# A recommender tower with embedding look-ups by matmul: the last two tables are looked up in batch halves

## The chip, the cores and the metric

One core of a Trainium2 chip runs the whole kernel. The metric is the device time of one execution in microseconds (us). The core has a tensor engine (PE, whose weight loads are shown apart as PEld), a vector engine (DVE), a scalar engine (ACT), GpSimd (POOL), and a sync engine (SP) that issues DMAs; they run side by side and wait for each other through semaphores.

## What is computed

For a batch of 512 items, 26 rows are looked up by id, one in each of 26 tables of 128 columns, and stacked with a dense vector of 128 values to 27 features. The products of all pairs of features (351 of them) and the dense vector go through three layers:

```python
e = jnp.stack([tbl_0[ids[:, 0]], ..., tbl_25[ids[:, 25]]], axis=1)
all_emb = jnp.concatenate([bottom_output[:, None, :], e], axis=1)
gram = jnp.einsum('bfd,bgd->bfg', all_emb, all_emb)
z = gram[:, _TRIU_I, _TRIU_J]
h = jnp.concatenate([z, r_bottom_output], axis=1)
h = jnp.maximum(h @ W_top1 + b_top1, 0.0)      # 479 -> 512
h = jnp.maximum(h @ W_top2 + b_top2, 0.0)      # 512 -> 256
y = h @ W_top3                                 # 256 -> 1
```

All is in float32.

## The kernel before

The batch is cut into four tiles of 128 items. `features` (in SBUF) holds for each item its 27 features, with the 128 columns on the partitions.

**Picked tables.** The twelve tables of 1000 rows (`PICKED`) are not gathered. SP loads each whole table in order (L175); ACT rounds it to `table_hi` (L319) and DVE subtracts that to get `table_lo` (L221). The look-up is a matmul with a one-hot matrix that DVE (L236, L239) and ACT (L322, L328) make from the ids: PE's `pick(i)` runs 8 matmuls of 512 columns with `table_hi` (L425) and 8 with `table_lo` (L434), all into one of two PSUM banks, and ACT's `pick_out` (L333) copies the bank to `features`. The tables are handled in couples that share a one-hot buffer. Buffers of `table_hi` and `table_lo` alternate, so that their writers wait for the pick two tables earlier (`picked_done`).

**Gathered tables.** The other fourteen tables are gathered row by row by POOL: for each tile, four groups (`TURNS`: 4, 4, 4 and 2 tables), one indirect DMA per table (L204), 56 in all, in the order of tiles. Gathers of tiles 2 and 3 reuse the buffers of tiles 0 and 1 and wait until those groups are turned. PE turns each group with transposes (`turn(t, g)`, L450), and ACT or DVE copies the result into `features` (L216). `AFTER_PICK` says behind which pick a turn stands in PE's order, `TAIL_TURNS` gives the order of the later ones; ACT copies the turns of `AFTER_PICK`, DVE those of the tail. The pair turns `("z", t)` of the tail are in the same numbering, since all turns share two PSUM banks.

**Products and layers.** `products(t, half)` runs two matmul instructions (27 columns) for each of 64 items of a tile (L463). When both halves are done, DVE transposes them in blocks (`grams_out`, L261 and L263), ACT takes the wanted pairs out (`bands_out`, L347), PE turns these (`pairs_turn`, L475), DVE copies them (L213), and the layers follow: `layer1` (L481), `layer2` (L501), `layer3` (L508), with ACT's copies (L352, L357, L362) behind each. A float32 matmul of the code is two matmul instructions on PE, each with its own weight load.

**Order.** Each engine runs its program in the order in which it is written out by hand; there is no planner. PE's order is at the end of the tensor block: the twelve picks with turns behind some of them, then products, turns, pair turns and layers interleaved. PE runs every instruction in that order.

Of the kernel before, what the change touches and what calls it, by code (L numbers as in the profile page):

```python
# [17 lines left out]
BIAS_ROW = CHUNK_ROWS  # L18
PICKED = [1, 2, 4, 5, 11, 13, 14, 16, 22, 23, 24, 25]
PICKS = len(PICKED)  # L20
COUPLES = PICKS // 2
GATHERED = [f for f in range(TABLES) if f not in PICKED]
ORDER = PICKED + GATHERED
PICK_ROWS = 1000
RPP = BIG_RPP = -(-PICK_ROWS // 128)
# [10 lines left out]
def rpp(i):  # L36
    return BIG_RPP if i // 2 in BIG_COUPLES else RPP
# [8 lines left out]
def dve_onehots(j):  # L46

    return sum((2 if k == 0 else 1) * (rpp(2 * k) - 1) for k in range(j))


def act_onehots(j):
    return sum(2 if k == 0 else 1 for k in range(j))


AFTER_PICK = {2: [(0, 0)], 3: [(0, 1)], 4: [(0, 2)], 5: [(0, 3)], 6: [(1, 0)], 8: [(1, 1)], 9: [(1, 2)], 10: [(1, 3)],
              11: [(2, 0)]}
TAIL_TURNS = [(2, 1), ("z", 0), (2, 2), (2, 3), (3, 0), ("z", 1), (3, 1), (3, 2), (3, 3), ("z", 2), ("z", 3)]
TURN_ORDER = [rows for i in range(PICKS) for rows in AFTER_PICK.get(i, [])] + TAIL_TURNS
PLACE = {what: n for n, what in enumerate(TURN_ORDER)}
BY_ACT = [n < len(TURN_ORDER) - len(TAIL_TURNS) for n in range(len(TURN_ORDER))]  # L60
# [3 lines left out]
def dlrm_tower(nc, bottom_turned, ids, picked_ids, picked, tables, w1, w2, b2, w3, out):  # L64
# [3 lines left out]
    with ExitStack() as ctx:  # L68
# [40 lines left out]
        pick_ps = mlp_ps  # L109
# [4 lines left out]
        def onehot_of(i, c):  # L114
            return onehot[i // 2 % 2][:, c, :, :]
# [103 lines left out]
        def _(dve):  # L219
# [31 lines left out]
            def turn_out(n):  # L251
                dve.wait_ge(turned, n + 1)
                copy_turned(nc.vector.tensor_copy, n).then_inc(turn_dve, 1)

            def grams_out(t):

                dve.wait_ge(prods_done, t + 1)
                by_second = prod_ps[t % 2][:].rearrange("p m c -> p c m")
                if t >= 1:
                    dve.wait_ge(bands_ready, 2 * t)  # L260
                nc.vector.transpose(grams[:, 0:FEATURES - 1, :], by_second[:, 1:FEATURES, :]  # L261
                                    ).then_inc(grams_ready, 1)
                nc.vector.transpose(grams[:, FEATURES - 1:, :], by_second[:, 0:BANDS, :]  # L263
                                    ).then_inc(grams_ready, 1)
# [8 lines left out]
            for i in range(PICKS):  # L273
                pick_operands(i)
            dve.wait_ge(fills_ready, 4)
            grams_out(0)
            turn_out(PLACE[(2, 1)])
            turn_out(PLACE[("z", 0)])
            grams_out(1)
            turn_out(PLACE[(2, 2)])  # L280
            turn_out(PLACE[(2, 3)])
            turn_out(PLACE[(3, 0)])
            turn_out(PLACE[("z", 1)])
            grams_out(2)
            turn_out(PLACE[(3, 1)])
            turn_out(PLACE[(3, 2)])
            turn_out(PLACE[(3, 3)])
            turn_out(PLACE[("z", 2)])
            grams_out(3)
            turn_out(PLACE[("z", 3)])  # L290

# [1 line left out]
        def _(act):  # L293
# [34 lines left out]
                    nc.scalar.activation(onehot[j % 2][:, 0, :, :], distance[:], ACT.Relu, bias=1.0, scale=-4.0  # L328
                                         ).then_inc(onehot_act, 1)

            def pick_out(i):
                act.wait_ge(picked_done, i + 1)
                nc.scalar.copy(features[:, :, 1 + i, :],  # L333
                               pick_ps[i % 2][:].rearrange("p a (b i) -> p (a b) i", i=2)
                               ).then_inc(picks_ready, 1)

            def turn_out(n):
# [30 lines left out]
            for i in range(PICKS + 2):  # L368
                if i < PICKS:
                    table_high(i)  # L370
# [5 lines left out]
                if 1 <= i <= PICKS:  # L376
                    pick_out(i - 1)
            act.wait_ge(fills_ready, 4)
            act.wait_ge(mlp_in, 48)
            act.wait_ge(onehot_act, act_onehots(COUPLES))  # L380
            bands_out(0)
            bands_out(1)
            h1_out(0, 0)
            h1_out(0, 1)
# [20 lines left out]

        @block.tensor
        def _(pe):
            def pick(i):

                if i == 0:  # L410
                    pe.wait_ge(first_hi_ready, 1)
                else:
                    pe.wait_ge(hi_ready, i + 1)
                if i >= 2:
                    pe.wait_ge(picks_ready, i - 1)
                acc = pick_ps[i % 2][:].rearrange("p a b -> p (a b)")
                for n, c in enumerate(places(i)):
                    if i == 0 and n == HALF:
                        pe.wait_ge(hi_ready, 1)
                    before = dve_onehots(i // 2) + (RPP - 1 if i == 1 else 0)  # L420
                    if c == 0:
                        pe.wait_ge(onehot_act, i + 1 if i < 2 else act_onehots(i // 2 + 1))
                    elif i % 2 == 0 or i == 1:
                        pe.wait_ge(onehot_ready, before + n + 1)
                    nc.tensor.matmul(acc, table_hi[i % 2][:, c, :], onehot_of(i, c)[:, i % 2, :],  # L425
                                     start=(n == 0), stop=False)
                if i == 0:
                    pe.wait_ge(first_lo_ready, 1)
                else:
                    pe.wait_ge(lo_ready, i + 1)  # L430
                for n, c in enumerate(places(i)):
                    if i == 0 and n == HALF:
                        pe.wait_ge(lo_ready, 1)
                    last = nc.tensor.matmul(acc, table_lo[i % 2][:, c, :], onehot_of(i, c)[:, i % 2, :],  # L434
                                            start=False, stop=(n == rpp(i) - 1))
                last.then_inc(picked_done, 1)

            def copied(n):
# [76 lines left out]
            for i in range(PICKS):  # L515
                pick(i)
                for rows_of in AFTER_PICK.get(i, []):
                    if rows_of == (0, 0):
                        pe.wait_ge(ident_ready, 1)
                    turn(*rows_of)  # L520
            pe.wait_ge(fills_ready, 4)
            pe.wait_ge(bottom_ready, 1)
            pe.wait_ge(picks_ready, PICKS)
            products(0, 0)
            products(0, 1)
            turn(2, 1)
            products(1, 0)
            pairs_turn(0)
            products(1, 1)
            turn(2, 2)  # L530
            turn(2, 3)
            pe.wait_ge(w1_in, 16 * (CHUNKS + 1))
            pe.wait_ge(mlp_in, 48)
            layer1(0)
            turn(3, 0)
            products(2, 0)
            pairs_turn(1)
            layer2(0)
            layer3(0)
            products(2, 1)  # L540
            turn(3, 1)
            layer1(1)
            turn(3, 2)
            turn(3, 3)
            products(3, 0)
            pairs_turn(2)
            layer2(1)
            layer3(1)
            products(3, 1)
            layer1(2)  # L550
            pairs_turn(3)
# [54 lines left out]
```

## Time and profile before

| | |
|---|---|
| timed runs | 142.22, 143.40, 146.07 us; median 143.4 |
| profiled execution | 139.8 us, span 138.0 us |
| PE busy | 101.3 us (73%), 1520 matmuls |
| PE weight loads busy | 84.2 us (61%) |
| DVE, ACT busy | 58.1 us (42%), 49.5 us (36%) |
| POOL busy | 62.6 us (45%), 56 gathers |
| HBM read | 15.00 MB, 109 GB/s over the span |

The profile is of one execution. Its own time is a little more than its span, which counts from the first to the last instruction. Busy times of engines overlap; an engine's busy share over the whole span says little where the kernel has stages. Matmuls are pipelined and the ends of their records are modelled, so that a mean duration of one matmul is more than what it adds to a sequence: for the pace, take the start of a group and the start of the next. "Issue" as what ended a wait means that the profile shows nothing that the engine waited for.

### The profile page before, as it was taken

The numbers are of one execution on the slowest core, as the hardware profiler recorded it, in microseconds if no ns is written. First come the engines' busy times: TensorE is split into PE (matmuls) and PEld (weight loads), VectorE is DVE, ScalarE is ACT, GpSimd is POOL, SyncE is SP. The second block draws the span as 40 slices with busy tenths as digits, with TensorE's granted clock in tenths as the row PEclk, the third lists the DMA queues.
The fourth block names the chain that finished last, engine by engine and source line by source line (L and its number), as shares of the span: only waits on it lengthen the run. The fifth ranks groups of instructions, "written<-read, shape, count | busy, mean of one in ns | idle before, by whom it ended". The sixth has DMA issues, their size and how long they took to land.

```text
span 138.0 us, 3425 instructions
## 1 busy us (share of the span) xinstructions
PE 101.3 (73%) x1520; PEld 84.2 (61%) x1520; DVE 58.1 (42%) x87; ACT 49.5 (36%) x79; POOL 62.6 (45%) x63
## 2 busy tenths in 40 slices
PE   6998989999999969942111111556599976999994
PEld 6965558888888848821101000455499876989792
DVE  5799999599798971000000000014172062141000
ACT  4449648779495991130000000003031222124222
POOL 2388787887888788778777773000000000000000
PEclk9999999999999999997555555557999999999999
DMA  4895987985983982112211221000000000000000
GB/s 68 301 416 199 318 276 226 274 301 189 229 322 108 329 285 62 46 57 57 57 45 50 57 57 38 5 5 0 5 5 5 5 0 5 5 5 0 5 0 1
DMA packets 6369, 15.23 MB, mean 110 GB/s; under 512 B 1745, under 2 KB 2257, under 8 KB 6354
## 3 DMA queue, kind: packets, MB, share of 16 engines
q1 hardware_dynamic: 4418, 11.07, 23.6%
q0 software_dynamic: 1792, 3.67, 9.6%
q10 hardware_dynamic: 144, 0.26, 1.3%
q8 instruction: 12, 0.20, 0.6%
q14 instruction: 3, 0.02, 0.0%
HBM read 15.00 MB, written 0.00 MB: 109 GB/s over the span
## 4 chain that ended last, share of the span: by engine, by line
PE 38%; issue 28%; POOL 22%; DMA 8%; ACT 1%; DVE 1%
POOL rows L204 22%; PE prod_ps L463 11%; PE mlp_ps L481 11%; PE mlp_ps L501 5%; DMA rows<-in_tbl_dram,ids_all 5%; PE turn_ps L450 3%; DMA ids_all<-in_ids_dram 3%; PE mlp_ps L425 3%; PE mlp_ps L434 3%; PE turn_ps L475 1%; ACT h L357 1%; PE mlp_ps L508 1%; DVE features L216 1%; ACT distance L362 0%
## 5 line engine op out<-in xcount | busy, mean ns | idle before, releaser
L204 POOL DMA_INDIRECT rows<-in_tbl_dram,ids_all x56 | 61.8, 1104 | 20.8 <-issue 16.8
L463 PE MATMUL prod_ps<-features 128*27 128x27 f32 x1024 | 16.4, 203 | 29.9 <-issue 28.8
L463 PEld LDWEIGHTS prod_ps<-features 128*27 128x27 f32 x1024 | 13.5, 117 | 33.1 <-issue 31.7
L425 PE MATMUL mlp_ps<-onehot,table_hi 128*128 128x512 f32 x96 | 26.2, 408 | 1.0 <-ACT table_hi L319 0.5
L261 DVE STREAM_TRANSPOSE grams<-prod_ps 128x832 f32<-128x832 f32 x4 | 4.2, 1050 | 49.3 <-PE prod_ps L463 49.3
L434 PE MATMUL mlp_ps<-onehot,table_lo 128*128 128x512 f32 x96 | 24.2, 394 | 0.4 <-issue 0.4
L239 DVE TENSOR_SCALAR onehot<-ids_wide,row_of 128x1024 fp32r<-128x1024 int32 x35 | 23.7, 746 | 0.0
L434 PEld LDWEIGHTS mlp_ps<-onehot,table_lo 128*128 128x128 f32 x96 | 17.8, 188 | 5.1 <-issue 1.1
L425 PEld LDWEIGHTS mlp_ps<-onehot,table_hi 128*128 128x128 f32 x96 | 17.1, 188 | 6.0 <-DVE onehot L239 1.7
L347 ACT COPY bands<-grams 128x117 f32<-128x117 f32 (+1 forms) x8 | 4.0, 506 | 44.6 <-DVE grams L261 44.3
L221 DVE TENSOR_TENSOR table_lo<-table_raw,table_hi 128x1024 fp32r<-128x1024 f32 (+1 forms) x13 | 14.6, 1134 | 3.9 <-issue 3.9
L319 ACT CAST table_hi<-table_raw 128x1024 fp32r<-128x1024 f32 (+1 forms) x12 | 12.1, 1011 | 4.4 <-DMA table_raw<-in_picked_dram 3.5
L333 ACT COPY features<-mlp_ps 128x512 f32<-128x512 f32 x12 | 7.9, 656 | 12.9 <-PE mlp_ps L434 7.0
L481 PE MATMUL mlp_ps<-pairs,w_sb 128*128 128x128 f32 x96 | 11.4, 275 | 0.0
L481 PEld LDWEIGHTS mlp_ps<-pairs,w_sb 128*128 128x128 f32 x96 | 11.0, 192 | 0.0
L450 PE MATMUL turn_ps<-ident,rows 128*128 128x128 f32 x56 | 9.1, 287 | 1.1 <-DMA rows<-in_tbl_dram,ids_all 1.1
L450 PEld LDWEIGHTS turn_ps<-ident,rows 128*128 128x128 f32 x56 | 6.9, 146 | 2.7 <-DMA rows<-in_tbl_dram,ids_all 1.6
L501 PE MATMUL mlp_ps<-h,w_sb 128*128 128x128 f32 x64 | 8.1, 277 | 0.0
L501 PEld LDWEIGHTS mlp_ps<-h,w_sb 128*128 128x128 f32 x64 | 7.5, 192 | 0.2 <-ACT h L352 0.2
L357 ACT ACTIVATE h<-mlp_ps,b_sb 128x128 f32<-128x128 f32 x8 | 2.9, 367 | 10.5 <-PE mlp_ps L501 10.5
L216 DVE COPY features<-turn_ps 128x512 f32<-128x512 f32 (+1 forms) x7 | 4.0, 600 | 5.7 <-PE turn_ps L450 5.7
L514 PE MATMUL turn_ps<-h 128*128 128x128 f32 x28 | 5.7, 393 | 1.1 <-DVE h L266 1.1
(32 smaller groups left out, 61.8 us busy)
## 6 DMA issues: line engine op xcount, KB each, us to landing
table_raw<-in_picked_dram SPq DMA_DIRECT2D x11, 512.0 KB
ids_wide<-in_picked_ids_dram SPq DMA_DIRECT2D x5, 512.0 KB
w_sb<-in_W_top_dram SPq DMA_DIRECT2D x4, 256.0 KB
rows<-in_tbl_dram,ids_all POOLq DMA_INDIRECT x56
table_raw<-in_picked_dram SPq DMA_DIRECT2D x2, 256.0 KB, 4.6
w_sb<-in_W_top_dram SPq DMA_DIRECT2D x1, 512.0 KB
ids_wide<-in_picked_ids_dram ACTq DMA_DIRECT2D x1, 256.0 KB, 4.4
ids_wide<-in_picked_ids_dram SPq DMA_DIRECT2D x1, 256.0 KB
```

The lines of the kernel that those rows point to most:

```text
L204: nc.gpsimd.indirect_dma_start(out=rows[t % 2][:, slot - FIRST_G, :], out_offset=None, in_=tables[table], in_offset=bass.IndirectOffsetOnA ...
L221: return nc.vector.tensor_tensor(table_lo[i % 2][:, begin:end, :], table_raw[i % RAWS][:, begin:end, :], table_hi[i % 2][:, begin:end, :]. ...
L239: nc.vector.tensor_scalar(onehot_of(i, c), ids_wide[j % 2][:], row, None, ALU.is_equal).then_inc(onehot_ready, 1)
L319: nc.scalar.copy(table_hi[i % 2][:, 0:end, :], table_raw[i % RAWS][:, 0:end, :]).then_inc(hi_ready, 1)
L333: nc.scalar.copy(features[:, :, 1 + i, :], pick_ps[i % 2][:].rearrange("p a (b i) -> p (a b) i", i=2)).then_inc(picks_ready, 1)
L425: nc.tensor.matmul(acc, table_hi[i % 2][:, c, :], onehot_of(i, c)[:, i % 2, :], start=(n == 0), stop=False)
L434: last = nc.tensor.matmul(acc, table_lo[i % 2][:, c, :], onehot_of(i, c)[:, i % 2, :], start=False, stop=(n == rpp(i) - 1))
L450: last = nc.tensor.transpose(turn_ps[n % 2][:, i, :], rows[t % 2][:, slot - FIRST_G, :], ident[:])
L463: last = nc.tensor.matmul(prod_ps[t % 2][32 * s:32 * s + FEATURES, m, 0:FEATURES], item, item, start=True, stop=True)
L481: return nc.tensor.matmul(mlp_ps[n // 2][:, n % 2, :], w1_sb[:, c, 128 * n:128 * n + 128], rhs, start=start, stop=stop, skip_group_check=True)
L501: last = nc.tensor.matmul(mlp_ps[m][:, 2, :], w2_sb[:, c, 128 * m:128 * m + 128], h1[:, c, :], start=(c == 0), stop=(c == 3))
L514: nc.tensor.matmul(turn_ps[0][:, 0, :], h1[:, 0, :], h1[:, 0, :], start=True, stop=True)
```

## The change

Of the twelve picks, the first ten stay whole. The last two are each cut into two halves of the batch (256 columns); the order of the parts is: table 10 first half, table 11 first half, table 10 second half, table 11 second half. `pick` becomes `pick_high` and `pick_low`, and the four pieces of the second halves (8 matmuls each) are spread: one ahead of the products of tile 0, the others between products of tiles 0 and 1. Three turns of tile 1 move one pick forward, the turn (2, 0) is now copied by DVE, and the turns of tile 3, the pair turns and the products (3, 0) change their places in the tail. Products (3, 0) now stand directly ahead of products (3, 1).

```diff
+WHOLE = PICKS - 2
+PARTS = [(i, 0, 2) for i in range(WHOLE)] + [(WHOLE, 0, 1), (WHOLE + 1, 0, 1), (WHOLE, 1, 2), (WHOLE + 1, 1, 2)]
+SIDE = 256
...
-AFTER_PICK = {2: [(0, 0)], 3: [(0, 1)], 4: [(0, 2)], 5: [(0, 3)], 6: [(1, 0)], 8: [(1, 1)], 9: [(1, 2)], 10: [(1, 3)],
-              11: [(2, 0)]}
-TAIL_TURNS = [(2, 1), ("z", 0), (2, 2), (2, 3), (3, 0), ("z", 1), (3, 1), (3, 2), (3, 3), ("z", 2), ("z", 3)]
+AFTER_PICK = {2: [(0, 0)], 3: [(0, 1)], 4: [(0, 2)], 5: [(0, 3)], 6: [(1, 0)], 7: [(1, 1)], 8: [(1, 2)], 9: [(1, 3)]}
+TAIL_TURNS = [(2, 0), (2, 1), ("z", 0), (2, 2), (2, 3), ("z", 1), (3, 0), (3, 1), ("z", 2), (3, 2), (3, 3), ("z", 3)]
...
@@ DVE @@
             dve.wait_ge(fills_ready, 4)
+            turn_out(PLACE[(2, 0)])
             grams_out(0)
...
-            turn_out(PLACE[(3, 0)])
             turn_out(PLACE[("z", 1)])
             grams_out(2)
+            turn_out(PLACE[(3, 0)])
             turn_out(PLACE[(3, 1)])
+            turn_out(PLACE[("z", 2)])
             turn_out(PLACE[(3, 2)])
             turn_out(PLACE[(3, 3)])
-            turn_out(PLACE[("z", 2)])
             grams_out(3)
@@ ACT @@
-            def pick_out(i):
-                act.wait_ge(picked_done, i + 1)
-                nc.scalar.copy(features[:, :, 1 + i, :],
-                               pick_ps[i % 2][:].rearrange("p a (b i) -> p (a b) i", i=2)
+            def pick_out(part):
+                i, begin, end = PARTS[part]
+                act.wait_ge(picked_done, part + 1)
+                nc.scalar.copy(features[:, SIDE // 2 * begin:SIDE // 2 * end, 1 + i, :],
+                               pick_ps[i % 2][:, 2 * begin:2 * end, :].rearrange("p a (b i) -> p (a b) i", i=2)
                                ).then_inc(picks_ready, 1)
...
+            pick_out(WHOLE + 1)
+            pick_out(WHOLE + 2)
             act.wait_ge(fills_ready, 4)
             act.wait_ge(mlp_in, 48)
             act.wait_ge(onehot_act, act_onehots(COUPLES))
             bands_out(0)
+            pick_out(WHOLE + 3)
             bands_out(1)
@@ PE @@
+            def acc(i, begin, end):
+                return pick_ps[i % 2][:, 2 * begin:2 * end, :].rearrange("p a b -> p (a b)")
+
+            def pick_high(part):
+                i, begin, end = PARTS[part]
...
+                if part >= 2:
+                    pe.wait_ge(picks_ready, part - 1)
...
+                    nc.tensor.matmul(acc(i, begin, end), table_hi[i % 2][:, c, :], onehot_of(i, c)[:, i % 2, SIDE * begin:SIDE * end],
+                                     start=(n == 0), stop=False, skip_group_check=True)
...
+            pick_high(WHOLE)
+            pick_low(WHOLE)
+            pick_high(WHOLE + 1)
+            pick_low(WHOLE + 1)
+            turn(2, 0)
+            pick_high(WHOLE + 2)
             pe.wait_ge(fills_ready, 4)
             pe.wait_ge(bottom_ready, 1)
-            pe.wait_ge(picks_ready, PICKS)
+            pe.wait_ge(picks_ready, WHOLE + 2)
             products(0, 0)
+            pick_low(WHOLE + 2)
             products(0, 1)
+            pick_high(WHOLE + 3)
             turn(2, 1)
             products(1, 0)
+            pick_low(WHOLE + 3)
             pairs_turn(0)
             products(1, 1)
             turn(2, 2)
             turn(2, 3)
...
+            pe.wait_ge(picks_ready, WHOLE + 4)
             layer1(0)
-            turn(3, 0)
             products(2, 0)
             pairs_turn(1)
             layer2(0)
             layer3(0)
             products(2, 1)
+            turn(3, 0)
             turn(3, 1)
             layer1(1)
+            pairs_turn(2)
             turn(3, 2)
             turn(3, 3)
-            products(3, 0)
-            pairs_turn(2)
             layer2(1)
             layer3(1)
+            products(3, 0)
             products(3, 1)
             layer1(2)
             pairs_turn(3)
```

## Rows read from the trace of the kernel before

**Rows 1.** The page's part 2: busy tenths of the span in 40 slices.

```profile
PE   6998989999999969942111111556599976999994
...
POOL 2388787887888788778777773000000000000000
PEclk9999999999999999997555555557999999999999
```

**Rows 2.** Busy time by stage: stretch, length, busy us (count) of each engine, granted clock.

```profile
core 0: us, PE busy (x) PEld busy (x) DVE busy (x) ACT busy (x) POOL busy (x), PEclk, DMA share, GB/s
59.40:88.40 29.00, 4.96 (x73) 3.16 (x73) 0.00 (x0) 0.35 (x1) 18.88 (x20) 0.58 0.18 48
88.40:100.70 12.30, 7.95 (x453) 7.01 (x454) 3.24 (x5) 1.04 (x2) 0.00 (x0) 0.75 0.02 5
100.70:138.00 37.30, 32.94 (x745) 29.96 (x743) 8.99 (x15) 10.03 (x26) 0.00 (x0) 1.00 0.01 3
```

**Rows 3.** The waits of PE: us in total, times, longest us.

```profile
PE prod_ps L463 <- issue: 28.8, 24, 2.6
```

**Rows 4.** PE's timeline: start us, us, what, count, idle before it.

```profile
45.34 2.10 PE L425 MATMUL mlp_ps<-onehot,table_hi 128*128 128x512 f32 x8
47.27 1.99 PE L434 MATMUL mlp_ps<-onehot,table_lo 128*128 128x512 f32 x8
50.40 0.66 PE L450 MATMUL turn_ps<-ident,rows 128*128 128x128 f32 x4 [1.14 <-DMA rows<-in_tbl_dram,ids_all]
50.81 2.09 PE L425 MATMUL mlp_ps<-onehot,table_hi 128*128 128x512 f32 x8
...
54.69 2.07 PE L425 MATMUL mlp_ps<-onehot,table_hi 128*128 128x512 f32 x8
...
59.43 0.49 PE L463 MATMUL prod_ps<-features 128*27 128x27 f32 x37 [0.41 <-issue]
...
85.59 0.20 PE L463 MATMUL prod_ps<-features 128*27 128x27 f32 x1 [2.59 <-issue]
...
88.39 1.92 PE L463 MATMUL prod_ps<-features 128*27 128x27 f32 x143 [0.46 <-issue]
91.73 0.69 PE L463 MATMUL prod_ps<-features 128*27 128x27 f32 x41 [1.41 <-issue]
92.35 1.12 PE L450 MATMUL turn_ps<-ident,rows 128*128 128x128 f32 x4
93.39 1.23 PE L463 MATMUL prod_ps<-features 128*27 128x27 f32 x82
95.92 0.60 PE L463 MATMUL prod_ps<-features 128*27 128x27 f32 x46 [1.29 <-issue]
...
96.96 0.86 PE L463 MATMUL prod_ps<-features 128*27 128x27 f32 x78
99.47 0.63 PE L463 MATMUL prod_ps<-features 128*27 128x27 f32 x50 [1.64 <-issue]
...
104.84 1.28 PE L463 MATMUL prod_ps<-features 128*27 128x27 f32 x128
...
109.10 1.26 PE L463 MATMUL prod_ps<-features 128*27 128x27 f32 x122
...
112.25 0.49 PE L481 MATMUL mlp_ps<-bottom_t,w_sb 128*128 128x128 f32 x3 [0.74 <-issue]
...
117.17 1.28 PE L463 MATMUL prod_ps<-features 128*27 128x27 f32 x128 [1.09 <-DVE features L216]
```

**Rows 5.** The chain that ended last, one piece, and POOL's timeline, last gather.

```profile
43.77 6.59 DMA rows<-in_tbl_dram,ids_all
83.25 0.94 POOL L204 DMA_INDIRECT rows<-in_tbl_dram,ids_all  x1 [0.30 <-issue]
```

**Rows 6.** DMA queues: whole span, then 58 to 89 us, then 89 to 90 us.

```profile
q8 instruction: 12, 0.20, 0.6%
...
q0 software_dynamic: 705, 1.44, 17.9%
...
q8 instruction: 1, 0.02, 5.8%
```

**Rows 7.** The chain again: lengths of layer 1, layer 2 and a pair turn.

```profile
118.45 0.52 PE turn_ps L475 x3
118.97 1.80 PE mlp_ps L501 x16
...
122.69 3.77 PE mlp_ps L481 x32
```

More of the change, by code:

```diff
@@ L367, in _ @@
             act.wait_ge(minus_row_ready, 1)
-            for i in range(PICKS + 2):
-                if i < PICKS:
-                    table_high(i)
+            for i in range(PICKS):
+                table_high(i)
                 if i == 3:
@@ L375, in _ @@
                     turn_out(PLACE[rows_of])
-                if 1 <= i <= PICKS:
+                if 1 <= i:
                     pick_out(i - 1)
+            pick_out(WHOLE + 1)
+            pick_out(WHOLE + 2)
             act.wait_ge(fills_ready, 4)
@@ L407, in _ @@
         def _(pe):
-            def pick(i):
+            def acc(i, begin, end):
+                return pick_ps[i % 2][:, 2 * begin:2 * end, :].rearrange("p a b -> p (a b)")
+            def pick_high(part):
+                i, begin, end = PARTS[part]
                 if i == 0:
                     pe.wait_ge(first_hi_ready, 1)
-                else:
+                elif begin == 0:
                     pe.wait_ge(hi_ready, i + 1)
-                if i >= 2:
-                    pe.wait_ge(picks_ready, i - 1)
-                acc = pick_ps[i % 2][:].rearrange("p a b -> p (a b)")
+                if part >= 2:
+                    pe.wait_ge(picks_ready, part - 1)
                 for n, c in enumerate(places(i)):
@@ L419, in pick, with pick_low @@
                         pe.wait_ge(hi_ready, 1)
-                    before = dve_onehots(i // 2) + (RPP - 1 if i == 1 else 0)
-                    if c == 0:
+                    ready = dve_onehots(i // 2) + (RPP - 1 if i == 1 else 0)
+                    if c == 0 and begin == 0:
                         pe.wait_ge(onehot_act, i + 1 if i < 2 else act_onehots(i // 2 + 1))
[L423 to L426, printed above, removed]
+                    elif begin == 0 and (i % 2 == 0 or i == 1):
+                        pe.wait_ge(onehot_ready, ready + n + 1)
+                    nc.tensor.matmul(acc(i, begin, end), table_hi[i % 2][:, c, :], onehot_of(i, c)[:, i % 2, SIDE * begin:SIDE * end],
+                                     start=(n == 0), stop=False, skip_group_check=True)
+            def pick_low(part):
+                i, begin, end = PARTS[part]
                 if i == 0:
                     pe.wait_ge(first_lo_ready, 1)
-                else:
+                elif begin == 0:
                     pe.wait_ge(lo_ready, i + 1)
@@ L433, in pick @@
                         pe.wait_ge(lo_ready, 1)
-                    last = nc.tensor.matmul(acc, table_lo[i % 2][:, c, :], onehot_of(i, c)[:, i % 2, :],
-                                            start=False, stop=(n == rpp(i) - 1))
+                    last = nc.tensor.matmul(acc(i, begin, end), table_lo[i % 2][:, c, :], onehot_of(i, c)[:, i % 2, SIDE * begin:SIDE * end],
+                                            start=False, stop=(n == RPP - 1), skip_group_check=True)
                 last.then_inc(picked_done, 1)
@@ L514, in _ @@
                 nc.tensor.matmul(turn_ps[0][:, 0, :], h1[:, 0, :], h1[:, 0, :], start=True, stop=True)
-            for i in range(PICKS):
-                pick(i)
+            for i in range(WHOLE):
+                pick_high(i)
+                pick_low(i)
                 for rows_of in AFTER_PICK.get(i, []):
```

## The prediction

> **What bounds the kernel now.** I read the time first: the profiled execution took 139.8 us, of which the span is 138.0 and 1.8 lies around it; the median of the three timed runs is 143.4, which is 3.6 above it. Any change of the span that I work out is added to 143.4.
>
> The slices of the page come next [rows 1]. TensorE (PE) is 80 to 90% busy up to slice 16, nearly idle in slices 17 to 24, and dense again to the end; its granted clock halves (2.4 to 1.2 GHz) inside that hole and comes back behind it. GpSimd (POOL) is busy until the hole is nearly over. The table by stage says the same in us [rows 2]: from 59.4 to 88.4 PE is busy for 5.0 of 29.0 us, with DVE and ACT idle; the stage 88.4 to 100.7 (products of tiles 0 and 1) is 65% busy at a mean clock of 0.75; from 100.7 on PE is busy for 32.9 of 37.3 us at the full clock. The waits of PE [rows 3] put 28.8 us on the products line, released by "issue", that is, by nothing that the profile shows.
>
> The timeline of PE shows how it begins [rows 4]. 37 matmuls of the first half of tile 0's products run in 0.49 us, then single matmuls or threes follow at distances of 0.7 us or multiples of it, down to one in 1.4 to 2.8 us, and at 88.39 suddenly 143 run in 1.92 us. All wait for nothing that another engine computes. I call this the **crawl**: 35 pairs of weight load and matmul in 28.5 us. It begins when ACT's last copies are done and it ends 4.2 us after POOL's last gather leaves its engine (83.25 + 0.94 = 84.19) [rows 5]. Between 58 and 89 us the DMA engines carry the gathers and nothing else [rows 6].
>
> Behind it is a second limit, visible at 90.3, 94.6, 97.8 and 111.5 us. Between two such gaps lie 41 + 4 + 82 = 127 matmuls, and 46 + 3 + 78 = 127 [rows 4]. With their weight loads that is about 256 instructions, and the instruction queue moved 12 packets for 0.20 MB, 16 KB each, one at 89 to 90 us [rows 6]. So PE's code comes in **blocks of 128 pairs**, and the next block is asked for when the present one starts. From the start of one block to that of the next it took 95.92 - 91.73 = 4.2, 99.47 - 95.92 = 3.6, and, counting 128 pairs back from 112.25 (5 + 4 + 119, a start near 109.1), about 3.1 us: mean 3.6. A half of a tile's products is one block (128 matmuls) and runs in 1.28 us, so pure products wait for code.
>
> **The change, part by part.** (1) *Turns brought forward.* The turn (1, 2) stands behind pick 8 instead of pick 9. Before, PE ended pick 9 at about 49.2 and waited until the last gather of that group had landed: issued at 43.77, landed 6.59 us later, at 50.36 [rows 5]. In the change PE ends pick 8 at 45.4, with the turn (1, 1) done ahead of it, and waits for the same rows until 50.4. Nothing on SP's or POOL's queue that delayed the landing is moved: POOL's gaps are its own 0.30 us [rows 5]. Pick 9 thus runs 50.8 to 54.7, where pick 10 ran. ACT's cast of table 11 waits for pick 9 and so ends about 5 us later, near 56.4, just ahead of its use at 56.8.
>
> (2) *Halves.* Whole picks take 3.9 us [rows 4]; a half is 16 matmuls of 256 columns, so 1.95 us if the time goes by columns. The bounds are 1.8 (16 x 0.11, the pace of 128-column pairs [rows 7]) and 3.9 (nothing saved); I take 1.95, the nearer kind being the 512-column row with its weight loads hidden. The two first halves end at 54.8 + 3.9 = 58.7, the turn (2, 0) at 59.1, the quarter ahead of the products (8 matmuls) at 60.1. Products begin at about 60.1 against 59.4: what the halves save, the wait in (1) takes.
>
> (3) *The crawl.* The burst of products that it begins with is the same and stands at the same time, the gathers are the same. I let it end at 88.4, with POOL, and with the same 72 pairs done. The cost of (1) and (2) is then nothing, hidden by the crawl; without that cover it is 0.7 us, or 2 us more if PE's clock falls in the 4.7 us wait of (1) and pick 9 runs at half pace.
>
> (4) *88.4 to 100.7.* Three quarters (24 pairs, 2.9 us at the full clock) are added. Block ends come 8 pairs earlier. The first block then holds 127 products and a quarter: at the low clock 127 x 13.4 ns (1.92 us / 143) + 1.9 = 3.6 us, ending at 92.0 instead of 91.7. The next two stay bound by their code, 3.6 us each, so the quarters lie in time that PE waited in before. Behind the third block 86 pairs remain to the layers instead of 54, 32 more, products at 10 ns: 0.3. I take +0.3; bounds 0 and +2.9 (nothing hidden).
>
> (5) *The tail.* Counting pairs from 88.4 (products 128, turns 4 or 2, pair turns 3, first layer 32, second 16, third 4 [rows 7]) I get block ends at 519, 647, 775, 903 and 1031. The block to 647 holds 118 products, 3 pair turns and 7 of layer 2, 2.5 us of work: 1.1 us of waiting. That to 775 has 3.0: 0.6. **The products of tile 3 now stand together**, so that the block 903 to 1031 is products alone: 1.3 us of work, 2.3 of waiting. Together 4.0 us. The order before has only the 0.74 us ahead of 112.25 (2.9 of work, so 0.7 by the same count). Term: +3.3, with the block time at 3.1 or 4.2 instead of 3.6: +2.3 to +4.5.
>
> (6) *The copy.* Before, products (3, 0) waited for DVE's copies of the last turns, 1.09 us idle ahead of 117.17 plus what PE lost in starting [rows 4]. Now two layers stand between: -1.2. Other moved copies (turn (2, 0) to DVE, the pair copies) have 2 us or more of PE work over them; if one were late it would be 0.7 us, a copy's length.
>
> Sum: 0.3 + 3.3 - 1.2 = **+2.4 us**, span 140.4, profiled 142.2; against the median 145.8, 1.7% more. With the bounds: +1.1 to +6.2, 144.5 to 149.6.
>
> What a page says against term (5): the Trainium skill, "Runtime: NRT & Kernel Launch", section "Instruction fetch mechanics", has the code refilled in blocks of 256 instructions while the present one runs, the crossing "mostly hidden". The block length agrees with the 127 pairs above; "hidden" doesn't, for stretches of products, by the gaps above.
>
> **Rivals.** *A, the forecast* (0.40): the crawl ends with POOL. For it: it ends just behind the last gather, and PE runs through far denser bursts afterwards. Against: gathers ran all along beside the picks without a crawl.
>
> *B, the crawl has a length of its own* (0.18), 28.6 us from its start, or ends so many instructions in. Then everything of (1) and (2) counts: +2.4 + 0.7, up to +2.4 + 2.7. Time 146.5 to 148.5, slower. It decides as soon as products start later than 59.4. For it: the crawl sits in one place of the code, 37 pairs into the products, and the records name no event that ends it.
>
> *C, the crawl is cut short or does not come* (0.30): its cause sits in how PE's code, its blocks and DVE's and ACT's idling meet there, and all of that is shifted by 16 instructions and one quarter. Without it the last gathers bind: they land at about 85.5, and behind the turn (3, 3) the change has 21 to 22 us of layers and products, so span 108, median 108 + 1.8 + 3.6 = 113. Cut to half, the tail from 88.4 starts some 14 us earlier: 132. I give 0.13 to its absence and 0.17 to values from 115 to 140.
>
> *D, the quarters do what they can* (0.12): the blocks come at the best pace seen or sooner, and term (5) is nothing: 0.3 - 1.2 = -0.9, time 142.5. Nothing in rows 4 speaks for it but the block at 112.25 being quicker than the others. It is where "mostly hidden" would lead.
>
> **How the numbers follow.** About 2% is what a measurement of this kernel tells from no change: 140.5 to 146.3. A lies astride the upper line: 0.23 within, 0.17 above. B is above (0.18). D is within (0.12). C is faster but for 0.01. So faster 0.29, same 0.36, slower 0.35. The time is A's, 145.8. A's own range is 144.5 to 149.6. For 8 in 10 the range must take in D and the half-cut crawls of C: 125 to 150, leaving out the absence of the crawl (0.13) and a little above.
>
> **What would show it.** PE waits from about 45.6 to 50.4 for rows (step 1). Products begin near 60 (2). A hole of single matmuls 0.7 us apart up to about 88.4 (3); its end moved with its start speaks for B. Pick matmuls of 256 columns at 89 to 98 with gaps of code behind the 127th pair (4). A gap of 2 to 2.5 us inside products (3, 1) and one inside layer 2 of tile 0 (5). No DVE wait ahead of products (3, 0) (6). I am wrong if the hole is missing or short, or if the products of tile 3 run without a gap.

## The result and the profile after

The changed kernel took 142.9 us (median of 12 runs, 141.2 to 144.9), the kernel before, run beside it, 142.3 (12 runs). The ratio, taken from the fast executions of each kernel alone, is **1.016 [1.010, 1.021]**: 1.6% slower, under the 2% that a measurement tells from no change, though its interval lies above 1. The medians of all 12 are only 0.4% apart, and a repeat (e10 below) gave 1.008, so that the size of the loss is known less well than the interval says. The forecast was 1.017. The profiled execution took 142.85 us with a span of 141.1, against 139.8 and 138.0: +3.1 of span where +2.4 was the sum.

The slices of the kernel after, from its page:

```profile
PE   6898889999989189970011011998898898499994
...
POOL 2388878878878787877777760000000000000000
PEclk9999999999999856997555555589999999959999
```

Counted from 0 as in [rows 1], the hole of PE ends with slice 24, as before, but behind it PE is at 8 or 9 where it was at 5 or 6. Two things are new in the clock: it falls in slices 13 to 15, ahead of the hole, and once more in slice 35.

The busy time by stage of the kernel after, cut at the same events as [rows 2] (end of the hole, start of layer 1 of tile 0), columns as there:

```profile
core 0: us, PE busy (x) PEld busy (x) DVE busy (x) ACT busy (x) POOL busy (x), PEclk, DMA share, GB/s
60.65:88.28 27.63, 4.18 (x44) 2.89 (x43) 0.69 (x1) 0.76 (x2) 17.92 (x19) 0.59 0.18 47
88.28:100.95 12.67, 11.50 (x520) 10.60 (x520) 3.39 (x5) 1.88 (x4) 0.00 (x0) 0.82 0.02 5
100.95:141.10 40.15, 34.49 (x745) 31.26 (x743) 8.82 (x15) 10.04 (x26) 0.00 (x0) 0.96 0.01 2
```

Against the stages of before (ends at 88.39, 100.74 and 138.0) the hole ends 0.1 us earlier, the stage of products is 12.67 instead of 12.35 (+0.3), and what follows is 40.15 instead of 37.26 (+2.9). The middle stage now has PE busy for 11.5 of its 12.7 us: the three quarters of picks and slower products fill what was waiting before.

The waits of PE, kernel after (us in total, times, longest):

```profile
PE prod_ps L474 <- issue: 26.5, 15, 8.9
PE turn_ps L461 <- DMA rows<-in_tbl_dram,ids_all: 3.6, 1, 3.6
...
PE turn_ps L461 <- DVE pairs L215: 0.3, 1, 0.3
```

The row for the products answers [rows 3]; the wait for rows was 1.14 us [rows 4] and is 3.6; DVE's copy ahead of products (3, 0) is gone from the list, and a small one for DVE's copy of a pair turn has come.

The timeline of the kernel after, PE with single rows of ACT, DVE and POOL (start, length, what, count, idle before it):

```profile
49.77 1.11 PE L461 MATMUL turn_ps<-ident,rows 128*128 128x128 f32 x4 [3.57 <-DMA rows<-in_tbl_dram,ids_all]
50.54 3.76 PE L433 MATMUL mlp_ps<-onehot,table_hi 128*128 128x512 f32 x8
54.10 2.50 PE L445 MATMUL mlp_ps<-onehot,table_lo 128*128 128x512 f32 x8
...
57.61 1.12 PE L445 MATMUL mlp_ps<-onehot,table_lo 128*128 128x256 f32 x8
...
60.65 0.60 PE L461 MATMUL turn_ps<-ident,rows 128*128 128x128 f32 x4
...
71.46 0.38 ACT L337 COPY features<-mlp_ps 128x256 f32<-128x256 f32 x1 [9.62 <-remote]
72.05 0.49 PE L474 MATMUL prod_ps<-features 128*27 128x27 f32 x20 [8.93 <-issue]
...
77.86 0.69 DVE L218 COPY features<-turn_ps 128x512 f32<-128x512 f32 x1 [18.33 <-remote]
...
83.12 0.94 POOL L206 DMA_INDIRECT rows<-in_tbl_dram,ids_all  x1 [0.30 <-issue]
...
88.28 1.42 PE L474 MATMUL prod_ps<-features 128*27 128x27 f32 x99 [0.45 <-issue]
...
95.87 0.80 PE L474 MATMUL prod_ps<-features 128*27 128x27 f32 x70 [0.42 <-issue]
...
99.42 0.89 PE L474 MATMUL prod_ps<-features 128*27 128x27 f32 x82 [0.74 <-issue]
...
106.93 1.72 PE L512 MATMUL mlp_ps<-h,w_sb 128*128 128x128 f32 x14 [0.29 <-issue]
...
110.93 0.33 PE L474 MATMUL prod_ps<-features 128*27 128x27 f32 x18 [0.50 <-issue]
...
112.12 1.06 PE L492 MATMUL mlp_ps<-bottom_t,w_sb 128*128 128x128 f32 x8
...
123.41 1.30 PE L474 MATMUL prod_ps<-features 128*27 128x27 f32 x90 [2.02 <-issue]
124.64 2.08 PE L492 MATMUL mlp_ps<-bottom_t,w_sb 128*128 128x128 f32 x8
```

Read it from the top. PE waits for the rows of (1, 2) until 49.8 and then does pick 9 in 3.76 + 2.50 us instead of about 2.1 + 2.0: the granted clock fell to its lower level (1.2 GHz) while PE stood still. (These are sums of record lengths; from its start to the start of what follows, pick 9 took 5.9 us, and 3.7 before.) Halves of 8 matmuls with 256 columns take 1.0 us from start to start. ACT's copy of the first half of pick 11, whose matmuls were done before 61, runs only at 71.46, and DVE's copy of the turn (2, 0), ready at 61.2, only at 77.86. **The crawl holds ACT and DVE as well as PE**, and this is why the products start at 72.05 and not near 60. What comes late is the sign that an engine waits for: the semaphore events of the trace have the sign of that pick at 71.4 and that of the turn at 77.8, each within 0.1 us of the copy that it lets go. POOL's last gather leaves at 84.06 and the crawl ends at 88.28, 4.2 us later, as it was in [rows 5]. In the tail, waits for code stand at 106.9, 110.9 and 123.4; behind the last, the first 8 matmuls of a layer 1 take 2.08 us instead of 1.06.

One plain fact is needed for what follows: the chips differ. On one of those used below none of the four profiles has the crawl, and the kernel before took 113.3 us there, against 139 to 142 on the others. Each ratio is against the kernel before on the same chip.

### The profile page after: what moved, and what is told of

Same layout as the page of the kernel before. It is cut to its first block, busy times and chain, and to the rows that moved or that the text cites. A ratio compares the mean times of both kernels' runs of the same rounds, so it can differ in the third digit from the quotient of the medians.

```text
span 141.1 us, 3491 instructions
## 1 busy us (share of the span) xinstructions
PE 103.6 (73%) x1552; PEld 87.4 (62%) x1552; DVE 58.9 (42%) x88; ACT 49.2 (35%) x80; POOL 62.7 (44%) x63
## 4 chain that ended last, share of the span: by engine, by line
PE 42%; issue 25%; POOL 22%; DMA 7%; ACT 1%; DVE 0%
POOL rows L206 22%; PE mlp_ps L492 11%; PE prod_ps L474 10%; PE mlp_ps L433 5%; PE mlp_ps L512 5%; PE mlp_ps L445 5%; DMA rows<-in_tbl_dram,ids_all 4%; PE turn_ps L461 3%; DMA ids_all<-in_ids_dram 3%; PE turn_ps L486 1%; ACT h L361 1%; PE mlp_ps L519 1%; DVE pairs L215 0%; ACT distance L366 0%
## 5 line engine op out<-in xcount | busy, mean ns | idle before, releaser
L474 PE MATMUL prod_ps<-features 128*27 128x27 f32 x1024 | 14.2, 204 | 26.5 <-issue 26.5
L433 PE MATMUL mlp_ps<-onehot,table_hi 128*128 128x512 f32 (+1 forms) x112 | 28.4, 393 | 2.3 <-issue 1.3
L474 PEld LDWEIGHTS prod_ps<-features 128*27 128x27 f32 x1024 | 12.1, 118 | 28.7 <-issue 28.4
L445 PE MATMUL mlp_ps<-onehot,table_lo 128*128 128x512 f32 (+1 forms) x112 | 26.3, 380 | 0.4 <-issue 0.4
L337 ACT COPY features<-mlp_ps 128x512 f32<-128x512 f32 (+1 forms) x14 | 8.1, 578 | 48.5 <-PE mlp_ps L445 37.0
L433 PEld LDWEIGHTS mlp_ps<-onehot,table_hi 128*128 128x128 f32 x112 | 19.4, 199 | 7.4 <-issue 1.9
L445 PEld LDWEIGHTS mlp_ps<-onehot,table_lo 128*128 128x128 f32 x112 | 20.2, 203 | 4.8 <-issue 1.1
L218 DVE COPY features<-turn_ps 128x512 f32<-128x512 f32 (+1 forms) x8 | 4.7, 610 | 18.4 <-remote 18.3
L215 DVE COPY pairs<-turn_ps 117x384 f32<-117x384 f32 x4 | 2.2, 558 | 12.1 <-PE turn_ps L486 12.1
L356 ACT ACTIVATE h<-mlp_ps 128x256 f32<-128x256 f32 x8 | 3.1, 384 | 9.2 <-PE mlp_ps L492 9.2
```

Of the source, the lines that this page charges most:

```text
L218: return engine_copy(dst, turn_ps[n % 2][:, 0:len(slots), :].rearrange("p f (b i) -> p f b i", i=2))
L337: nc.scalar.copy(features[:, SIDE // 2 * begin:SIDE // 2 * end, 1 + i, :], pick_ps[i % 2][:, 2 * begin:2 * end, :].rearrange("p a (b i) -> ...
L433: nc.tensor.matmul(acc(i, begin, end), table_hi[i % 2][:, c, :], onehot_of(i, c)[:, i % 2, SIDE * begin:SIDE * end], start=(n == 0), stop= ...
L445: last = nc.tensor.matmul(acc(i, begin, end), table_lo[i % 2][:, c, :], onehot_of(i, c)[:, i % 2, SIDE * begin:SIDE * end], start=False, s ...
L474: last = nc.tensor.matmul(prod_ps[t % 2][32 * s:32 * s + FEATURES, m, 0:FEATURES], item, item, start=True, stop=True)
```

## The experiments

Theory: the crawl ends when POOL has no gather left to issue, whatever PE does (T1), and the tail's order costs what its waits for code say (T2). Rivals: the crawl has a length of its own, or sits at a piece of PE's code (R1); it comes from the ring of descriptors that POOL's gathers are written to (R2); from the start of the products (R3); or from gathers piling up (R4).

**e1_ring27 and e2_after_ring27: a ring of 27 KB** for the kernel before and the one after; h1, the bands and the warm-up's operand are put elsewhere to make room.

```diff
-        h1 = sb("h1", [128, HID1 // 128, TILE])
+        h1 = distance[:, 1, :].rearrange("p (c n) -> p c n", n=TILE)
...
-    nc = _bacc.Bacc("TRN2", target_bir_lowering=False, num_devices=1)
+    nc = _bacc.Bacc("TRN2", target_bir_lowering=False, num_devices=1, dynamic_dma_scratch_size=27648)
```

> The kernel before with 27,648 instead of 16,384 bytes per partition for the descriptor ring of the gathers (h1 and bands are laid into buffers that are free by then). Ring theory: in both traces the crawl begins with the 37th gather (59.53 us before, 58.76 after), as if that many had filled the ring once and every later one needed something that slows all sequencers. 27,648 holds 1.69 times as much, 60 gathers, more than the 56: no crawl, POOL ends near 84 as before, and the last gathers bind: span 138.0 minus up to 28, so 108 to 113, ratio near 0.80. Company theory (the crawl comes from gathers beside idle engines or beside products, whatever their number): unchanged, ratio 1.00. Own-length theory: unchanged too.

> The changed kernel with the same larger ring. Ring theory: ACT's, DVE's and PE's waits of 3 to 16 us between 58.6 and 88.3 go; products start near 62 and the last gathers, near 84, bind; behind turn (3, 3) it has 21 to 22 us of work; ratio to the kernel before 0.78 to 0.82. Against e1: quarters now cost PE 2.9 us where nothing hides them, but the gathers hide most; within 2 us of e1. Company theory: ratio 1.016 as measured.

Measured: 143.1 us, ratio 1.004 [0.997, 1.011], and 143.5, ratio 1.011 [1.004, 1.017]. Both have the crawl. In e2 it ends at 89.16, with POOL done at 84.93. In e1 it lay *among the picks*:

```profile
52.59 0.60 PE L452 MATMUL turn_ps<-ident,rows 128*128 128x128 f32 x4
57.44 2.94 PE L427 MATMUL mlp_ps<-onehot,table_hi 128*128 128x512 f32 x8 [4.25 <-issue]
...
73.44 0.60 ACT L335 COPY features<-mlp_ps 128x512 f32<-128x512 f32 x1 [16.06 <-remote]
73.74 0.94 POOL L206 DMA_INDIRECT rows<-in_tbl_dram,ids_all  x1 [3.84 <-remote]
...
76.07 3.43 PE L427 MATMUL mlp_ps<-onehot,table_hi 128*128 128x512 f32 x8 [7.92 <-ACT table_hi L321]
```

(Timeline of e1: PE, with single rows of ACT and POOL.) POOL's engine fell idle at 69.9, and ACT came free at 73.4, 3.5 us later. POOL was not short of a free row buffer: its next group, (3, 1), needs the turn (1, 1), which PE had done at 53.2 (first row), while the semaphore event of a turn that lets POOL go on stands at 73.5 to 73.7. POOL's sign came late like ACT's, so that this pause belongs to the crawl. It was the same in e3 (turn done at 67.5, POOL going on at 73.2) and in e9 (41.1 and 66.7). So a crawl needs neither products nor a fixed place in the code.

**e3_ring8: the kernel before with a ring of 8 KB**, the same line with 8192.

> The kernel before with half the ring, 8,192 bytes per partition. Ring theory: the crawl begins with the 19th gather, near 28 to 30 us, instead of the 37th, and lasts to POOL's end: the picks, which need ACT and DVE, crawl too; the span grows by tens of us, to over 160. Company theory and own-length theory: no change beyond 2%.

Measured in one execution: 142.2 us. Its timeline, PE and POOL:

```profile
51.46 3.78 PE L425 MATMUL mlp_ps<-onehot,table_hi 128*128 128x512 f32 x8 [9.85 <-ACT table_hi L319]
...
73.24 0.95 POOL L204 DMA_INDIRECT rows<-in_tbl_dram,ids_all  x1 [4.69 <-remote]
74.38 3.78 PE L425 MATMUL mlp_ps<-onehot,table_hi 128*128 128x512 f32 x8 [6.93 <-ACT table_hi L319]
...
88.50 0.95 POOL L204 DMA_INDIRECT rows<-in_tbl_dram,ids_all  x1 [0.30 <-issue]
...
90.38 1.69 PE L463 MATMUL prod_ps<-features 128*27 128x27 f32 x176 [0.31 <-issue]
```

The crawl lay at 41 to 72.8 (ACT's next copy, at 72.79) and ended 4.2 us after POOL's pause began (68.56). Behind it picks ran without being held beside gathers until 88.5. The ring's size neither brings nor removes it: R2 falls.

**e4_pause: POOL waits for tile 0's first products** ahead of the 33rd gather.

```diff
+                    if (t, g) == (2, 1):
+                        pool.wait_ge(prods_done, 1)
```

> The kernel before; POOL waits ahead of its 33rd gather (group (2, 1)) until the products of tile 0 are done. Ring theory: the products of tile 0 run without a crawl (59.4 to about 63, one wait for code), gathers 33 to 36 run beside products or layers without one, and the crawl begins with the 37th, near 68, and lasts until POOL is done near 63 + 24 x 1.25 + 4 = 97. Company theory: the crawl begins as soon as POOL goes on, near 63. Own-length theory: the crawl begins at 59.9 with the products and POOL, which waits for them, starts near 88. Span by the first two 143 to 148, by the third 165 or more.

Measured in one execution: 142.4 us. Timeline, PE and POOL:

```profile
59.74 2.00 PE L465 MATMUL prod_ps<-features 128*27 128x27 f32 x215 [0.41 <-issue]
64.13 0.55 PE L465 MATMUL prod_ps<-features 128*27 128x27 f32 x41 [2.39 <-issue]
65.47 0.94 POOL L206 DMA_INDIRECT rows<-in_tbl_dram,ids_all  x1 [13.61 <-PE prod_ps L465]
...
91.27 0.26 PE L465 MATMUL prod_ps<-features 128*27 128x27 f32 x2 [2.60 <-issue]
...
94.19 0.94 POOL L206 DMA_INDIRECT rows<-in_tbl_dram,ids_all  x1 [0.30 <-issue]
99.02 0.89 PE L465 MATMUL prod_ps<-features 128*27 128x27 f32 x55 [0.49 <-issue]
```

All of tile 0's products ran without a crawl while POOL was quiet: R3 falls. With the gathers it came, from 74 on, and ended at 99.02, 3.9 us after POOL's last (95.13). This is the run that moves the end by moving the gathers.

**e5_throttle and e6_42_gathers.** In e5 POOL waits, ahead of each gather, for the one two before it to have landed; e6 leaves out tile 3's 14 gathers (the second piece below), and the turns of tile 3 take the rows of tile 1.

```diff
+                        if len(issued) >= 2:
+                            pool.wait_ge(*issued[-2])
...
-            for t in range(TILES):
+            for t in range(TILES - 1):
```

> The kernel before; POOL waits ahead of each gather until the one two before it has landed (two semaphores per group, used in turn). The first four experiments showed the crawl at other places (41 to 73 us, 57 to 74, 74 to 99), on ACT and DVE too, each time ending 3.7 to 4.4 us after POOL ran out of gathers to run. Backlog theory: POOL's sequencer runs up to 12 gathers ahead of its engine, and this backlog makes the crawl: with two at most ahead there is none, and the span falls to 108 to 118. POOL-run theory without the backlog (gathers running without a break make it): it stays and ends 4 us behind the last gather; span 138 to 145. Own-length theory: 138.

> The kernel before without the 14 gathers of tile 3 (its rows are those of tile 1, so the output of tile 3 is not the reference's). POOL-run theory: POOL ends 14 x 1.25 = 17.5 us earlier, near 67, the crawl ends near 71, and the rest takes the 50 us as before: span 120 to 122. Own-length theory: span 138. If the crawl does not come at all: under 115.

Both met the chip without the crawl: the kernel before took 113.3 us. e5 took 142.7, ratio 1.279 [1.267, 1.290]: POOL's stream then ends at 114 us and PE waits for rows, with no crawl in it. That shows what a slower stream of gathers costs and nothing on R4, which stays open. e6 took 113.2 in one execution: without the crawl the 14 gathers of tile 3 are hidden.

**e12_42_again: e6's kernel on a chip with the crawl.**

> The kernel before without the gathers of tile 3 (the output of tile 3 isn't the reference's), the same kernel as e6_42_gathers, hoped to meet the crawl this time. POOL's last gather then leaves its engine some 11 x 1.24 us earlier, near 70 us. Theory 'the crawl ends with POOL's gathers': if the kernel before beside it runs at 142, PE's single matmuls 0.7 us apart end about 4 us behind that last gather, near 74, and since nothing else binds, the whole takes some 14 us less: 126 to 130. Rival 'the crawl ends when a fixed piece of PE's code or a fixed time is done': the end stays at 88.4 and the time at 140 to 143. If the kernel before runs at 113 here, there is no crawl and nothing is decided: the time is 113.

Measured in one execution: 137.9 us, beside 139.1 for the kernel before. Its timeline:

```profile
40.93 1.98 PE L434 MATMUL mlp_ps<-onehot,table_lo 128*128 128x512 f32 x8
...
62.59 0.95 POOL L204 DMA_INDIRECT rows<-in_tbl_dram,ids_all  x1 [0.30 <-issue]
...
67.16 0.60 ACT L333 COPY features<-mlp_ps 128x512 f32<-128x512 f32 x1 [9.31 <-remote]
...
83.33 2.00 PE L463 MATMUL prod_ps<-features 128*27 128x27 f32 x215 [0.41 <-issue]
```

The last gather left at 63.54, and ACT was free 3.6 us later. The end follows POOL, as T1 has it. But e9 below, with all 56 gathers, also has an early crawl, which ended at 66.4 in a pause of POOL; so e12 supports the 4 us behind POOL and doesn't show that fewer gathers end a crawl sooner. The time expected, 126 to 130, was a miss: this crawl had *begun* at about 41, not at 59, so the earlier end cut nothing off. Which of the two places a run takes is not set by the number of gathers.

**e7_new_tail and e8_after_old_tail: the two halves of the change by themselves**, on the chip without the crawl. e7 is the kernel before with the changed order behind layer 1 of tile 0 (its main lines below, the copies and TAIL_TURNS to match); e8 is the kernel after with that part undone.

```diff
-            turn(3, 0)
             products(2, 0)
...
             products(2, 1)
+            turn(3, 0)
             turn(3, 1)
             layer1(1)
+            pairs_turn(2)
...
-            products(3, 0)
-            pairs_turn(2)
             layer2(1)
             layer3(1)
+            products(3, 0)
             products(3, 1)
```

> The kernel before with the tail of the change alone (turns of tile 3, pair turns and products (3, 0) moved; picks whole, early turns as before). By the sum on record terms (5) and (6): +3.3 - 1.2 = +2.1 us, ratio 1.015 (1.007 to 1.023), with a gap of 2 us inside products (3, 1). By rival D (code hidden): -1.2 us, 0.992.

> The changed kernel with the tail of the kernel before: early turns, halves and quarters stay. By the sum on record what is left is the +0.3 us of term (4): ratio 1.002 (0.995 to 1.010), as the late start of the products is hidden by the crawl's end, which POOL sets. By rival B (crawl of its own length) 0.7 to 2.7 us more: 1.007 to 1.021.

Measured: e7 1.012 [1.001, 1.023], as expected; e8 0.988 [0.976, 1.001], under the range that was expected and with an interval that takes in 1. PE's timeline of e7:

```profile
58.05 3.15 PE L463 MATMUL prod_ps<-features 128*27 128x27 f32 x215 [0.41 <-issue]
...
71.69 1.06 PE L481 MATMUL mlp_ps<-bottom_t,w_sb 128*128 128x128 f32 x8
...
95.61 0.70 PE L463 MATMUL prod_ps<-features 128*27 128x27 f32 x58 [2.37 <-issue]
```

and of e8:

```profile
49.59 0.66 PE L461 MATMUL turn_ps<-ident,rows 128*128 128x128 f32 x4 [3.81 <-DMA rows<-in_tbl_dram,ids_all]
50.00 2.89 PE L433 MATMUL mlp_ps<-onehot,table_hi 128*128 128x512 f32 x8
...
61.04 1.59 PE L474 MATMUL prod_ps<-features 128*27 128x27 f32 x128
...
74.87 1.06 PE L492 MATMUL mlp_ps<-bottom_t,w_sb 128*128 128x128 f32 x8
...
91.19 1.28 PE L474 MATMUL prod_ps<-features 128*27 128x27 f32 x128 [1.10 <-DVE features L218]
```

e7's row at 95.61 is the gap in the products of tile 3, 2.37 us; e8 has DVE's 1.10 there instead. Where no crawl covers it, the wait for rows with the fall of the clock makes e8's products start 3.0 us later than e7's (61.04 against 58.05), and layer 1 of tile 0 3.2 later. In these two profiles the spans come out alike (111.6 for e7, 112.0 for e8) while the timed ratios differ by 2.4%; runs on this chip spread from 110 to 118 us, the medians of all runs are 114.3 and 113.8 beside 113.3 for the kernel before, and one profile of each doesn't settle it.

**e10_after, e11_after_old_tail and e9_combined: the same parts with the crawl.** e10 is the kernel after once more, e11 is the same kernel as e8. e9 goes on from e11: the turns (1, 1), (1, 2), (1, 3) and (2, 0) stand later, where their rows should have landed (the last three below; DVE copies them), and the pair turn of tile 2 stands ahead of products (3, 0).

```diff
             pick_high(WHOLE)
             pick_low(WHOLE)
+            turn(1, 2)
             pick_high(WHOLE + 1)
             pick_low(WHOLE + 1)
-            turn(2, 0)
+            turn(1, 3)
...
             pick_low(WHOLE + 2)
+            turn(2, 0)
             products(0, 1)
```

> The changed kernel as it is, beside the same kernels. On a chip with the crawl: ratio 1.016 again. On one without it the two parts measured apart (new tail 1.012, halves with early turns 0.988) should add up to 1.000 (0.990 to 1.010).

> e8 again. Without the crawl 0.988 again: quarters between products use time in which PE waits for code. With the crawl: the sum on record has +0.3 us here, 1.002, and the gap to e10 is the tail's, 1.2 to 1.5%.

> The changed kernel with the tail of the kernel before and late turns: (1, 1) behind pick 8, (1, 2) behind the first half of table 10, (1, 3) behind that of table 11, (2, 0) behind products (0, 0), all three copied by DVE; the pair turn of tile 2 ahead of products (3, 0). On a chip without the crawl (before at 113): the wait for rows ahead of (1, 2), 3.8 us in e8, goes, products start near 55 instead of 58.1 (before) and 61.0 (e8), and most of that stays: 108 to 110, ratio 0.955 to 0.975. On a chip with the crawl (before at 142): the crawl ends with POOL whatever stands before it, so only the tail counts: ratio 0.99 to 1.005.

Measured, beside 141.8 for the kernel before: e10 143.2 us, ratio 1.008 [1.003, 1.014]; e11 140.4, **0.991 [0.986, 0.996]**; e9 140.8, 0.998 [0.994, 1.003]. e10 was expected at 1.016 again and e11 at 1.002: both came out lower, by 0.8 and 1.1%, and their distance, expected at 1.2 to 1.5%, is 1.7%. The last stage of e10, and then that of e11 with the two ahead of it (busy time by stage):

```profile
101.41:140.10 38.69, 33.09 (x745) 29.89 (x743) 8.82 (x15) 10.05 (x26) 0.00 (x0) 1.00 0.01 3
```

```profile
57.77:87.39 29.62, 5.86 (x70) 2.98 (x69) 0.00 (x0) 0.00 (x0) 19.39 (x21) 0.56 0.18 48
87.39:100.27 12.88, 11.31 (x482) 10.39 (x483) 3.41 (x5) 1.87 (x4) 0.00 (x0) 0.81 0.03 5
100.27:137.60 37.33, 33.00 (x745) 29.91 (x743) 8.93 (x15) 10.06 (x26) 0.00 (x0) 1.00 0.01 3
```

With the clock at 1.00 in both, the new tail is 38.69 - 37.33 = 1.4 us longer for the same busy time, so all of it is waiting. T2 holds, at 1.4 us in the profiles and 1.008 / 0.991 = 1.017 in the times, 2.4 us. The tail is what makes the change slower, and without it the change is a small gain over the kernel before (0.9%, under the 2%, with an interval below 1): of the versions with all gathers, e11 is the fastest on chips with the crawl. e9's crawl came early (41 to 69), so its late turns were not tried where the wait for rows is bare, on a chip without the crawl.

The wait for rows is no fixed price of the early turns. e11 has the same picks and turns as the kernel after up to the products, and PE's timeline has, at the turn (1, 2):

```profile
46.51 0.66 PE L461 MATMUL turn_ps<-ident,rows 128*128 128x128 f32 x4 [0.58 <-DMA rows<-in_tbl_dram,ids_all]
```

The rows were there at 46.5 and not at 49.8, a second wait (1, 3) took 1.34 us, the clock did not fall, and products started at 57.77, 1.7 us *earlier* than in the kernel before. Over the profiles with early turns this wait ran from 0.6 to 4.2 us (e10: 4.24).

## Why the prediction came out right, and where it was off

*Steps (1) and (2), turns and halves.* PE's wait for rows was forecast from 45.6 to 50.4 and lay at about 46.2 to 49.8. The clock did fall in it, which the prediction had as a possibility of 2 us; pick 9 took 5.9 us from start to start instead of 3.7. A half took about 2.0 us (forecast 1.95). The price of 0.7 to 2.7 us without cover was 3.0 in the profile of e8 against that of e7, but the wait behind it is not fixed: where the rows landed sooner (e11) products started earlier than before.

*Step (3), the crawl ends with POOL.* Held for every long crawl. From the end of POOL's last gather before quiet or a pause to that of the crawl: 4.2 us (before, after and e2), 3.5 (e1), 3.7 (e9, e10), 4.2 (e3), 3.9 (e4), 3.6 (e12), 4.1 (87.39 - 83.26, e11). In e1, e3 and e9 POOL's pause belongs to the crawl, so that these three show the order and not what ends it; e4, which moved the gathers, and the crawls that ended behind POOL's very last gather carry the theory. What counts is POOL's engine and not what is left to issue: in the kernel after POOL's sequencer had gone past its last gather by 69.1 us, where the trace has the start of the DRAIN behind it, and twelve gathers ran after that. Two short second crawls at the products, of 1.4 us in e1 and 5.0 in e9, ended 1.1 us behind POOL's last gather (88.44 - 87.31 and 90.23 - 89.10), which the theory doesn't explain. What failed is that the burst of products begins it and that ACT and DVE are merely idle: they are held too, and products started at 72.05 instead of 60.1. It cost nothing, since the end is POOL's.

*Step (4), the quarters.* +0.3 forecast, 12.67 - 12.35 = +0.3 measured in the profile. e10 and e11 have 13.2 and 12.9 us there, so it is within 0.9. In part two errors cancel: 72 pairs were to be done ahead of this stage and only 29 were, so 43 more products, about 0.5 us, had to be done in it, and the waits for code in it (0.42 and 0.74 us, against 1.41, 1.29 and 1.64 before [rows 4]) shrank by that much more.

*Step (5), waits for code in the tail: the term that was mis-sized.* Forecast 1.1 in layer 2 of tile 0, 0.6 behind it and 2.3 in products (3, 1), less 0.7 before: +3.3. Measured 0.29, 0.50 and 2.02, less 0.74: +2.1 (e10 against e11: 0.57, 0.22 and 2.02, less 0.70, again +2.1). The long gap was right in place and nearly in size; the two others came out at under half of what was forecast together. A page's rule was set against this term: the Trainium skill, "Runtime: NRT & Kernel Launch", section "Instruction fetch mechanics", has the crossing of a block "mostly hidden". In this profile the rows come near it where layers stand in the block (0.29 us), though the kernel with the old tail waited up to 1.31 us there in e1, and they do not agree with it for a block of nothing but small products (2.02, 2.37).

*Step (6), DVE's copy.* Forecast -1.2; the 1.09 us are gone and 0.30 at DVE's copy of a pair turn is new: -0.8. Steps (5) and (6) together give +1.3 where +2.1 was forecast, and e10 against e11 has 1.4. The profiled execution of the kernel after shows +2.9 because the clock fell at the end of the 2.02 us gap: 2.08 for 1.06, and 1.30 us for 90 products at the half clock (e10: 0.96). That fall, worth 40.15 - 38.69 = 1.5 us, is absent in e10, whose mean clock there is 1.00; it was not forecast.

*The sum.* That 1.016 meets 1.017 is in part luck. The tail (steps 5 and 6) was forecast at +2.1 and costs +1.4 in the profiles without the fall of the clock; the profile after has +3.1 in all only because that fall adds 1.5. The repeats, 1.008 and, of e2 to e1, 1.007, are half the forecast. In time the forecast 145.8 stood on a median of 143.4 from three executions; beside the kernel after the median was 142.3, and the measured 142.9 lies in the range for 8 in 10 (125 to 150) and below A's own (144.5 to 149.6). By the parts on the chip of e10, the halves give -0.9% (forecast +0.2%) and the tail takes +1.7% (forecast +1.5%, 2.1 of 143.4). **The gain of the halves is not located.** In e11's profile the crawl ends 1.0 us earlier than before, and POOL ended 0.9 us earlier too, with the same 56 gathers; POOL's end varies from 83.3 to 84.9 between profiles with nothing changed for it, so this may be chance. The stage behind is 0.5 us longer. No row shows 1.2 us.

*The rivals.* B (a length of its own, R1) fell: with the same picks and turns ahead of it the crawl ended at 87.4, 88.3 and 88.2 where PE's last unhindered work had ended at 58.2 (e11), 61.3 (after) and 62.6 (e10), that is, after 29, 27 and 26 us; 29 products were done in it in the kernel after and 72 before; and the end moved with POOL's gathers to 99 in e4. C did not happen through the change: both kernels have the crawl on the same chips. Its number, 113 us, is nevertheless what a chip without it shows, 113.3, for the kernel *before*. D fell by the 2.02 us gap, though its time, 142.5, is nearer to the measured one than A's. What starts the crawl, what delays the signs in it, why one chip has none, and why it sometimes begins at 41 us stays open; R4 was not decided.

## What to carry to other kernels

Before a schedule is tuned around a hole, profile it on other chips too, to see whether the hole belongs to the code: this one began at 41, 59 or 74 us, or not at all, and 29 of 142 us hung on it (142.3 - 113.3), twelve times the sum of this change. Small matmuls standing together for more than one block of code wait for their code, and layers or turns between them shorten that wait (0.2 to 0.6 us in the new tail), so an order that frees one DVE wait of 1.1 us can lose 2.0 us of code. A turn brought forward to where its rows haven't landed costs the wait and the clock behind it, which a hole elsewhere may hide on one chip and not on another (3.0 us in one profile here, nothing in another where the rows landed 3 us sooner).

## What the runs showed of the hardware that was not expected

PE, ACT and DVE are held together for 21 to 32 us, products being let through singly or a few at a time at multiples of 0.7 us (in e3 and e12 also 15 matmuls of a pick in a row), while POOL's gathers that are already on their way go on every 1.25 us as elsewhere; 3.5 to 4.2 us after POOL's engine falls idle all of them run on. The signs between engines come late in it: the turn (2, 0) of the kernel after ended at 61.2 and its semaphore event stands at 77.8, and POOL itself was held by such a late sign in e1, e3 and e9. The same kernel took 139 to 142 us on the chips where this happens and 113 on the one where it doesn't. Behind a wait of 3.6 us PE's granted clock was on its lower level (slices 13 to 15), and the 16 matmuls took 5.9 us from start to start instead of 3.7; at the wait of 2.0 us it fell in two profiles (after, e2) and not in a third (e10), nor at the 2.4 us of e7.
